# GNN layer pair on one core: attribute sums on GpSimd for the whole first half, GpSimd's share of the one-hots from set 44 on, and x's pieces and second half moved

## The chip, the cores and the metric

One Trainium2 chip, one core. The time is device microseconds of that core, the median of several executions; less is better. Engines: PE (TensorE, matmuls), PEld (its weight loads), DVE (VectorE), ACT (ScalarE), POOL (GpSimd), SP (SyncE, which issues DMAs).

## The reference

The inputs are x (3125 nodes, 64 channels), 53125 edges (src, dst, one attribute each) sorted by dst, and the weights of two message-passing layers. Cut to what matters:

```python
def _mp_layer(x, src, dst, edge_attr, W, b):
    loops = jnp.arange(n)
    src2, dst2 = concat([src, loops]), concat([dst, loops])
    ea2 = concat([edge_attr, zeros(n)])
    msg = concat([x[dst2], x[src2], ea2], axis=1) @ W + b
    return relu(segment_sum(msg, dst2, num_segments=n))
h = relu(_mp_layer(x, ..., W1, b1))
out = log_softmax(_mp_layer(h, ..., W2, b2))
return layernorm(x + out)
```

Since the message is linear, a layer needs, for each node, the sum of its neighbours' rows (an adjacency matrix times x), its degree, and the sum of the attributes of its edges.

## The kernel before

The 3125 nodes are 25 groups of 125. The adjacency matrix is built on the chip as 625 windows, each a 128x125 by 128x125 product on PE of two one-hot matrices made from the keys of 5 nodes' edges. Windows go in 79 **sets** of 8 (the last has one). One set is: DVE writes the one-hots of the set into one of three buffers `oh` (`onehots(k)`, L569: one compare of `iota_bank`, which lies in PSUM, with `keys`); PE builds the 8 windows in one of two PSUM buffers (`build(k)`, L1057); ACT copies them to the band of `adj` (`evacuate(k)`, L909). `build(k)` waits for set k-2's evacuation, `onehots(k)` for `build(k-3)`. PE runs four sets ahead: in its block b it does `build(b + 4)` and then layer 1's eight matmuls of set b (`layer1`, L1079). The order of all engines' work is written out by hand, by the set or block number.

Some work stands between the sets. When a group's 25 windows are summed, DVE reduces them (`reduce_sums`, L601); for each three groups there is an epilogue through the PSUM bank `epb`, started at the blocks in `TURN` (`turn_sums`, `hidden`, `messages` on PE; their copies on ACT; `scale_x`, `z_rest`, `z_low` on DVE). Layer 2 (L1126) starts when layer 1 is done, and needs nothing but PE and the final work on DVE.

What the change touches:

- **Shared one-hots.** From set `SHARED_FROM` = 12 on, DVE makes the one-hots of seven windows of a set (16 x 126 columns become 14 x 126) and GpSimd those of the eighth (`last_onehot`, two instructions of L441). PE waits for it ahead of the eighth matmul.
- **Attribute sums.** 625 blocks of edges are held as 125 rows by 5 columns j. For each j, DVE makes five masked sums (`attr_sums`, L556: one instruction with accumulation each), at the sets in `SUM_SET`. They need the distances `d_f` of that j, which ACT makes (`distances`, at the blocks in `DIST_BLOCK`). SP stores the five sums to DRAM and loads them turned (L1258, L1261), GpSimd splits them in bf16 parts (`split_sums`, at the sets in `SPLIT_BLOCK`), and `turn_sums` on PE waits for them (`se_parts`): for part 1 at block 21, part 2 at 29, part 3 at 41, part 4 at 60, part 5 at 69.
- **x's pieces.** Layer 1 takes x as three bf16 pieces: high (`cast_x`, ACT), middle (`rest_of_x` on DVE, then `cast_middle_x` on ACT), low (`low_of_x`, DVE). This is done for two halves of the groups, 12 and 13. Layer 1's first matmul waits for the first half's low piece, the thirteenth for the second half's.
- **Gathers.** GpSimd issues five indirect DMAs for the edges (L400) and five for the attributes (L404), each when its offsets are known (`off_ready`).
- **The bias rows** are split in three parts as well (`cast_bias`, `bias_rest`), and nine small DMAs on SP (L1253) copy them to their place; in SP's order they stand ahead of the first store of attribute sums.

## Time and profile before

| | |
|---|---|
| median of 3 runs | 193.68 us (193.29 to 193.81) |
| the profiled execution | 193.38 us, of which the span of its instructions is 191.3 us |
| PE busy | 173.1 us (90%) |
| PEld busy | 157.6 us (82%) |
| DVE busy | 161.4 us (84%) |
| ACT busy | 114.1 us (60%) |
| POOL busy | 98.6 us (52%) |
| mean granted clock of PE | 0.979 of full speed |

Busy times are instructions' spans. PE's matmuls are pipelined and their ends are modelled, so that the start of one instruction to the start of the next tells more than a length; the same holds for GpSimd. Times in rows are from the span's start. The profiled execution takes 2.1 us more than its span, and is 0.3 us below the median.

### The profile page before, as it was taken

Reading aid. Unit: us, or ns where it says so; the run is one execution under the profiler, and the core shown is the slowest. Engines: PE = TensorE matmul, PEld = TensorE weight load, DVE = VectorE, ACT = ScalarE, POOL = GpSimd, SP = SyncE. Lnnn points to the kernel's source line nnn. Section 1 sums busy time; section 2 is a strip of 40 time slices with the busy share of each in tenths; the row PEclk is TensorE's granted clock in tenths of the full one; section 3 lists DMA queues with packets and bytes.
Section 4 is the critical chain, followed back from the end, with each engine's and each line's share of the span. In section 5 each row is a group of like instructions: output and inputs, shape, how many; then the busy total and the mean of one; then the engine's idle time right before and its main releaser. Section 6 shows DMA issues by size and latency. Waiting matters only on the chain.

```text
span 191.3 us, 5193 instructions
## 1 busy us (share of the span) xinstructions
PE 173.1 (90%) x2050; PEld 157.6 (82%) x2051; DVE 161.4 (84%) x407; ACT 114.1 (60%) x197; POOL 98.6 (52%) x192
## 2 busy tenths in 40 slices
PE   7686587999999999999999999999999999999940
PEld 2133376998899987999999999999999999999930
DVE  0989999999999999999979979729429969888773
ACT  2526897888888989999989989863311102012201
POOL 6388504799889988988999989500000000000000
PEclk9969999999999999999999999999999999999995
DMA  1336200000000000000000000000000010200010
GB/s 45 103 90 146 65 11 2 6 1 4 1 6 1 4 1 4 2 4 1 3 0 3 2 3 0 3 0 5 0 3 2 16 27 0 44 13 17 20 25 20
DMA packets 9032, 3.35 MB, mean 18 GB/s; under 512 B 8240, under 2 KB 8557, under 8 KB 9007
## 3 DMA queue, kind: packets, MB, share of 16 engines
q1 hardware_dynamic: 8207, 2.08, 5.3%
q0 software_dynamic: 800, 0.93, 2.2%
q8 instruction: 17, 0.28, 0.7%
q14 instruction: 8, 0.07, 0.1%
HBM read 2.18 MB, written 0.81 MB: 16 GB/s over the span
## 4 chain that ended last, share of the span: by engine, by line
PE 64%; DVE 26%; DMA 5%; issue 3%; ACT 1%; DVEq 0%
PE pset L1126 18%; PE acc L1079 18%; DVE oh L569 16%; PE pset L1057 11%; PE acc L1126 9%; PE epb L1109 3%; PE epb L1120 3%; DMA adj<-in_edges,adj 3%; DMA adj<-in_dst 2%; DVE adj L556 1%; PE epb L1097 1%; DVE u L601 1%; DVE adj L581 1%; DVE x L586 1%; PE epb L1111 1%
## 5 line engine op out<-in xcount | busy, mean ns | idle before, releaser
L441 POOL TENSOR_SCALAR oh<-iota,keys 128x125 bf16<-128x125 bf16 x132 | 78.2, 615 | 14.9 <-PE pset L1057 14.3
L909 ACT ACTIVATE adj<-pset 125x1000 bf16<-125x1000 f32 (+1 forms) x79 | 78.4, 996 | 10.0 <-PE pset L1057 7.2
L569 DVE TENSOR_TENSOR oh<-iota_bank,keys 128x1764 bf16<-128x1764 bf16 (+4 forms) x81 | 83.1, 1051 | 0.4 <-PE pset L1057 0.3
L1079 PE MATMUL acc<-x,adj 125*125 125x195 bf16 x625 | 65.4, 248 | 0.3 <-DVE x L586 0.3
L1079 PEld LDWEIGHTS acc<-x,adj 125*125 125x125 bf16 x625 | 54.7, 136 | 0.9 <-issue 0.5
L1057 PE MATMUL pset<-oh 128*128 128x125 bf16 x625 | 47.3, 218 | 6.8 <-DVE oh L569 4.8
L1057 PEld LDWEIGHTS pset<-oh 128*128 128x128 bf16 x625 | 38.6, 97 | 10.4 <-ACT adj L909 6.1
L1126 PE MATMUL pset<-z,adj 125*125 125x192 bf16 x425 | 36.8, 246 | 0.0
L1126 PEld LDWEIGHTS pset<-z,adj 125*125 125x125 bf16 x425 | 35.5, 136 | 0.1
L988 ACT ACTIVATE x<-x 125x192 f32<-125x192 f32 (+2 forms) x6 | 2.6, 427 | 32.4 <-DVE x L737 32.4
L1126 PE MATMUL acc<-z,adj 125*125 125x192 bf16 x200 | 17.5, 246 | 0.0
L1126 PEld LDWEIGHTS acc<-z,adj 125*125 125x125 bf16 x200 | 16.8, 136 | 0.0
L601 DVE TENSOR_REDUCE u<-acc 125x65 f32<-125x195 f32 x25 | 8.9, 354 | 6.9 <-PE acc L1079 6.7
L1027 PE MATMUL acc<-adj 128*128 128x512 bf16 x31 | 11.3, 526 | 1.2 <-DVE adj L492 1.2
L1027 PEld LDWEIGHTS acc<-adj 128*128 128x128 bf16 x32 | 4.0, 127 | 6.5 <-issue 4.4
L400 POOL DMA_INDIRECT adj<-in_edges,adj x5 | 6.3, 1270 | 4.6 <-DVE adj L519 3.3
L728 DVE TENSOR_REDUCE x<-pset 125x64 f32<-125x192 f32 x17 | 5.4, 351 | 3.5 <-PE pset L1126 3.4
L556 DVE SCALAR_TENSOR_TENSOR adj<-adj 125x128 bf16<-125x128 f32 x25 | 7.4, 297 | 0.0
L404 POOL DMA_INDIRECT adj<-in_edge_attr,adj x5 | 6.1, 1211 | 1.5 <-issue 1.5
L1109 PE MATMUL epb<-turn,w1c 128*128 128x375 f32 x16 | 6.8, 506 | 0.0
L1120 PE MATMUL epb<-w2c,turn 128*125 128x128 f32 x48 | 6.7, 277 | 0.0
L622 DVE TENSOR_TENSOR u<-epb,z 125x192 f32<-125x192 f32 (+1 forms) x9 | 3.0, 338 | 4.1 <-ACT z L936 4.1
(125 smaller groups left out, 150.5 us busy)
## 6 DMA issues: line engine op xcount, KB each, us to landing
x_nat<-in_x_tiles SPq DMA_DIRECT2D x1, 406.2 KB
x_nat<-in_x_tiles SPq DMA_DIRECT2D x1, 375.0 KB
out<-x SPq DMA_DIRECT2D x2, 187.5 KB
out<-x SPq DMA_DIRECT2D x3, 93.8 KB
adj<-in_dst SPq DMA_DIRECT2D x1, 208.5 KB
bw<-adj SPq DMA_DIRECT2D x9, 1.0 KB
out<-x SPq DMA_DIRECT2D x1, 125.0 KB
adj<-in_edges,adj POOLq DMA_INDIRECT x5, 4.9
```

The lines of the kernel that those rows point to most:

```text
L400: gp.indirect_dma_start(pairs[:, j, 0:2 * (SLOTS - LOOPS)], None, edges, bass.IndirectOffsetOnAxis(off_idx[:, j:j + 1], 0)).then_inc(pairs ...
L441: ins = gp.tensor_scalar(oh[k % 3][:, OWN, side, 0:Q], iota1[:, 0:Q], keys[:, place(k * SET + OWN), side, 0:1], None, ALU.is_equal)
L556: dve.scalar_tensor_tensor(out=se_junk[:, j * WD + r, :], in0=d_f[:, j, :], scalar=float(r), in1=attrs[:, j, :], op0=ALU.is_equal, op1=ALU ...
L569: ins = dve.tensor_tensor(out=oh[k % 3][:, at_w:at_w + m, :, 0:2 * PAIRS].rearrange("p w t (q e) -> p (w t) q e", e=2), in0=iota_p.unsquee ...
L601: dve.tensor_reduce(u[i % 2][:, m, C:2 * C + 1], acc[g % 2][0:Q, 0:XW].rearrange("p (t c) -> p c t", t=3), AX.X, ALU.add)\
L909: ins = act.activation(bands[c][0:Q, :, at_w:at_w + n * WD].rearrange("p h (w e) -> p h w e", e=WD), rows[:, 0:n, 0:WD * G].rearrange("p w ...
L1027: pe.matmul(acc[1][:, :], still[:, 0:128], still, start=True, stop=True)
L1057: ins = pe.matmul(pset[k % 2][:, i // 4, i % 4 * 128:i % 4 * 128 + WD * G], oh[k % 3][:, i, 0, :], oh[k % 3][:, i, 1, 0:Q], start=True, st ...
L1079: ins = pe.matmul(acc[g % 2][0:Q, 0:XW], block_of_adj(g, h), x3[:, h, 0:XW], start=(h == 0), stop=(h == G - 1))
L1109: pe.matmul(epb[:, 0, 0:n], w1c[:, :], flat(i)[:, 0:n], start=True, stop=False)
L1120: ins = pe.matmul(z_cols(b - a)[:, m, :], flat(i)[:, m * Q:(m + 1) * Q], w2c[:, :], start=True, stop=True)
L1126: ins = pe.matmul(bank2(g)[0:Q, :], block_of_adj(g, h), z3[:, h, :], start=(h == 0), stop=(h == G - 1))
```

## The change

GpSimd makes all attribute sums. For each j it makes five masks, multiplies all of them with the attributes, and halves the 5 x 128 products seven times; a semaphore (`mask_chain`) orders each step behind the one before. Its share of the one-hots begins with set 44 in place of 12, behind all sums and splits in its program; until then DVE makes whole sets. GpSimd also makes the low piece of x's first half, and the rest and the low piece of the second half, between its gathers. SP asks for x's second half when the third offset is known, ahead of the weights, not when the first gather has landed. ACT casts the second half ahead of its first evacuation, its middle piece ahead of the third one, and makes `q_f` for j = 0, which was DVE's. The bias parts move to later sets, and two of ACT's `distances` four blocks forward.

```diff
-DIST_BLOCK = {1: 2, 2: 14, 3: 28, 4: 34}
-SUM_SET = {0: 16, 1: 24, 2: 31, 3: 37, 4: 43}
+DIST_BLOCK = {1: 2, 2: 14, 3: 24, 4: 30}
-SHARED_FROM = 12
+SHARED_FROM = 44
-SPLIT_BLOCK = {0: 26, 1: 34, 2: 44, 3: 52, 4: 60}
@@ gpsimd
+            def rest_of_x(i, a, b):
...
+                gp.wait_ge(xs_ready, i + 1)
+                gp.tensor_tensor(x_rest[:, a:b, :], x_nat[:, a:b, :], x3[:, a:b, 0:C], ALU.subtract).then_inc(xs_rest, 1)
...
+            def low_of_x(i, a, b):
...
+                gp.wait_ge(xm_ready, i + 1)
+                gp.tensor_tensor(x3[:, a:b, 2 * XC:2 * XC + C], x_rest[:, a:b, :], x3[:, a:b, XC:XC + C], ALU.subtract)\
+                  .then_inc(xl_ready, 1)
...
             gather_edges(0)
+            gather_edges(1)
             gather_attrs(0)
-            gather_edges(1)
-            gather_attrs(1)
-            for j in range(2, J):
-                gather_edges(j)
-            for j in range(2, J):
+            low_of_x(0, 0, XA)
+            rest_of_x(1, XA, G)
+            gather_edges(2)
+            low_of_x(1, XA, G)
+            gather_edges(3)
+            gather_edges(4)
+            for j in range(1, J):
                 gather_attrs(j)
...
+            def attr_sums(j):
+                gp.wait_ge(attrs_in[j], 16)
+                if j:
+                    gp.wait_ge(dist_ready, j)
+                    gp.wait_ge(se_ready, j)
+                else:
+                    gp.wait_ge(key_ready, 1)
+                for r in range(WD):
+                    gp.tensor_scalar(se_mask[:, r, :], d_f[:, j, :], float(r), None, ALU.is_equal).then_inc(mask_chain, 1)
+                done = j * (WD + 7) + WD
+                gp.wait_ge(mask_chain, done)
+                gp.tensor_tensor(se_mask, se_mask, attrs[:, j:j + 1, :].broadcast_to([Q, WD, SLOTS]), ALU.mult).then_inc(mask_chain, 1)
+                for n in (64, 32, 16, 8, 4, 2):
+                    done += 1
+                    gp.wait_ge(mask_chain, done)
+                    gp.tensor_tensor(se_mask[:, :, 0:n], se_mask[:, :, 0:n], se_mask[:, :, n:2 * n], ALU.add).then_inc(mask_chain, 1)
+                gp.wait_ge(mask_chain, done + 1)
+                gp.tensor_tensor(se_w[:, j, :], se_mask[:, :, 0], se_mask[:, :, 1], ALU.add).then_inc(se_ready, 1)
+
+            attr_sums(0)
+            for j in range(J):
+                if j + 1 < J:
+                    attr_sums(j + 1)
+                split_sums(j)
             for k in range(NSETS):
-                for j in range(J):
-                    if k == SPLIT_BLOCK[j]:
-                        split_sums(j)
                 if shared(k):
                     last_onehot(k)
@@ vector
-            bias_rest(0)
...
-            low_of_x(0, 0, XA)
             onehots(4)
-            rest_of_x(1, XA, G)
...
-                if k == 6:
-                    low_of_x(1, XA, G)
-                if k == 9:
+                if k == 10:
+                    bias_rest(0)
+                if k == 14:
                     bias_rest(1)
...
-                for j in range(J):
-                    if 0 <= k - SUM_SET[j] < WD:
-                        attr_sums(j, k - SUM_SET[j], k - SUM_SET[j] + 1)
@@ scalar
-            cast_bias(0)
             cast_x(0, 0, XA)
+            act.wait_ge(pairs_in[0], 16)
+            act.wait_ge(loops_ready, 2)
+            act.activation(q_f[:, 0, :], pairs[:, 0, 0::2], ACT.Copy, scale=1.0 / Q, bias=-float(Q // 2) / Q).then_inc(q0_ready, 1)
...
+            cast_x(1, XA, G)
             evacuate(0)
             evacuate(1)
-            cast_x(1, XA, G)
+            cast_middle_x(1, XA, G)
...
-                if b == 0:
-                    cast_middle_x(1, XA, G)
                 if b == 2:
+                    cast_bias(0)
+                if b == 8:
                     cast_bias(1)
-                if b == 6:
+                if b == 12:
                     cast_bias(2)
@@ sync
             sp.dma_start(x_nat[:, 0:XA, :], x_tiles[:, 0:XA, :]).then_inc(xnat_in[0], 16)
+            sp.wait_ge(off_ready, 3)
+            sp.dma_start(x_nat[:, XA:G, :], x_tiles[:, XA:G, :]).then_inc(xnat_in[1], 16)
             sp.dma_start(w1c[:, :], W1[0:2 * C, :]).then_inc(w_in, 16)
...
-            sp.wait_ge(pairs_in[0], 16)
-            sp.dma_start(x_nat[:, XA:G, :], x_tiles[:, XA:G, :]).then_inc(xnat_in[1], 16)
...
-                    sp.wait_ge(se_ready, (j + 1) * WD)
+                    sp.wait_ge(se_ready, j + 1)
```

How the order of instructions moves is seen at three places. On GpSimd, behind the constants, stood in a row before (L400 edges, L404 attributes, L441 the shared one-hots):

```order
L400 DMA adj<-in_edges,adj 125x246 [waits off_ready]
L404 DMA adj<-in_edge_attr,adj 125x123
L400 DMA adj<-in_edges,adj 125x246 [waits off_ready]
L404 DMA adj<-in_edge_attr,adj 125x123
L400 DMA adj<-in_edges,adj 125x246 [waits off_ready] x3
L404 DMA adj<-in_edge_attr,adj 125x123 x3
L441 TENSOR_SCALAR oh<-iota,keys 128x125 [waits keys_ready,built]
```

Now there stand (L415 low piece, L410 rest of x, L468 to L477 one j's attribute sums):

```order
L400 DMA adj<-in_edges,adj 125x246 [waits off_ready] x2
L404 DMA adj<-in_edge_attr,adj 125x123
L415 TENSOR_TENSOR x<-adj,x 125x12x64 [waits xm_ready]
L410 TENSOR_TENSOR adj<-x_nat,x 125x832 [waits xs_ready]
L400 DMA adj<-in_edges,adj 125x246 [waits off_ready]
L415 TENSOR_TENSOR x<-adj,x 125x13x64 [waits xm_ready]
L400 DMA adj<-in_edges,adj 125x246 [waits off_ready] x2
L404 DMA adj<-in_edge_attr,adj 125x123 x4
L468 TENSOR_SCALAR adj<-adj 125x128 [waits key_ready,attrs_in0]
L468 TENSOR_SCALAR adj<-adj 125x128 x4
L471 TENSOR_TENSOR adj<-adj 125x640 [waits mask_chain]
```

Three passes over x have come between the gathers, and the sums follow where the shared one-hots began.

On GpSimd at set 44, before: a `split_sums` (L423 to L431) between shared one-hots of one set and the next.

```order
L441 TENSOR_SCALAR oh<-iota,keys 128x125
L423 CAST stats<-se 125x5x3 [waits se_in2]
L425 TENSOR_TENSOR se_rest<-se,stats 125x5 [waits se_chain]
L427 CAST stats<-se_rest 125x5x3 [waits se_chain]
L429 TENSOR_TENSOR se_rest<-se_rest,stats 125x5 [waits se_chain]
L431 CAST stats<-se_rest 125x5x3 [waits se_chain]
L441 TENSOR_SCALAR oh<-iota,keys 128x125 [waits built]
```

Now the last two splits (L437 to L445) stand ahead of the first shared one-hot, set 44's (L455):

```order
L437 CAST stats<-se 125x5x3 [waits se_in3]
L439 TENSOR_TENSOR se_rest<-se,stats 125x5 [waits se_chain]
L441 CAST stats<-se_rest 125x5x3 [waits se_chain]
L443 TENSOR_TENSOR se_rest<-se_rest,stats 125x5 [waits se_chain]
L445 CAST stats<-se_rest 125x5x3 [waits se_chain]
L437 CAST stats<-se 125x5x3 [waits se_in4]
L439 TENSOR_TENSOR se_rest<-se,stats 125x5 [waits se_chain]
L441 CAST stats<-se_rest 125x5x3 [waits se_chain]
L443 TENSOR_TENSOR se_rest<-se_rest,stats 125x5 [waits se_chain]
L445 CAST stats<-se_rest 125x5x3 [waits se_chain]
L455 TENSOR_SCALAR oh<-iota,keys 128x125 [waits keys_ready,built]
```

The wait for the fifth load (`se_in4`) is now ahead of every shared one-hot.

On ACT, around the first evacuations, before (L860 bias cast, L864 `cast_x`, L880 and L882 the keys, L868 `cast_middle_x`, L909 evacuation):

```order
L860 ACTIVATE adj<-adj 64x128 [waits b_in]
L864 ACTIVATE x<-x_nat 125x12x64 [waits xnat_in0]
L880 ACTIVATE keys<-acc 128x125x2 [waits keyt_done]
L882 ACTIVATE keys<-acc 128x125x2
L868 ACTIVATE x<-adj 125x12x64 [waits xs_rest]
L909 ACTIVATE adj<-pset 125x25x40 [waits built] x2
L864 ACTIVATE x<-x_nat 125x13x64 [waits xnat_in1]
L909 ACTIVATE adj<-pset 125x25x40 [waits built] x3
L868 ACTIVATE x<-adj 125x13x64 [waits xs_rest]
```

Now (L878 `cast_x`, L888 `q_f`, L898 and L900 the keys, L882 `cast_middle_x`, L927 evacuation):

```order
L878 ACTIVATE x<-x_nat 125x12x64 [waits xnat_in0]
L888 ACTIVATE adj<-adj 125x128 [waits loops_ready,pairs_in0]
L898 ACTIVATE keys<-acc 128x125x2 [waits keyt_done]
L900 ACTIVATE keys<-acc 128x125x2
L882 ACTIVATE x<-adj 125x12x64 [waits xs_rest]
L878 ACTIVATE x<-x_nat 125x13x64 [waits xnat_in1]
L927 ACTIVATE adj<-pset 125x25x40 [waits built] x2
L882 ACTIVATE x<-adj 125x13x64 [waits xs_rest]
L927 ACTIVATE adj<-pset 125x25x40 [waits built] x5
```

The cast of x's second half now waits ahead of the first evacuation, and the cast of its middle piece, which waits for GpSimd's pass L410, ahead of the third.

## Rows read from the trace of the kernel before

**Rows 1.** Busy time of each engine by stage: window, length, busy us (instructions), clock, DMA.

```profile
16.70:50.00 33.30, 27.16 (x355) 24.50 (x357) 33.10 (x55) 27.03 (x34) 21.99 (x35) 1.00 0.11 24
50.00:76.00 26.00, 25.55 (x316) 23.38 (x315) 25.54 (x65) 23.66 (x43) 23.16 (x45) 1.00 0.04 3
76.00:129.00 53.00, 53.00 (x697) 51.26 (x696) 45.48 (x80) 46.88 (x74) 42.74 (x83) 1.00 0.02 2
```

**Rows 2.** Waits in 16 to 76 us: engine and line, releaser, total us, times, longest.

```profile
PEld pset L1057 <- ACT adj L909: 6.1, 7, 1.6
PE pset L1057 <- DVE oh L569: 4.8, 11, 0.8
```

**Rows 3.** Timeline of PE: start, length, line, tile [idle before it]; the builds of sets 24, 44 and 45.

```profile
50.30 0.60 PE L1057 MATMUL pset<-oh 128*128 128x125 bf16 x8
...
80.17 0.60 PE L1057 MATMUL pset<-oh 128*128 128x125 bf16 x8
...
81.29 0.60 PE L1057 MATMUL pset<-oh 128*128 128x125 bf16 x8
```

**Rows 4.** Timeline of DVE, 14.8 to 20.8 us and 34 to 41 us.

```profile
14.79 0.29 DVE L593 TENSOR_TENSOR adj<-adj 64x128 f32<-64x128 f32 x1
...
15.38 4.55 DVE L569 TENSOR_TENSOR oh<-iota_bank,keys 128x2016 bf16<-128x2016 bf16 x4
19.84 0.98 DVE L586 TENSOR_TENSOR x<-adj,x 125x768 bf16<-125x768 f32 x1
20.75 1.19 DVE L569 TENSOR_TENSOR oh<-iota_bank,keys 128x2016 bf16<-128x2016 bf16 x1
...
34.49 3.03 DVE L569 TENSOR_TENSOR oh<-iota_bank,keys 128x1764 bf16<-128x1764 bf16 x3
...
39.33 1.06 DVE L569 TENSOR_TENSOR oh<-iota_bank,keys 128x1764 bf16<-128x1764 bf16 x1
...
40.53 1.06 DVE L569 TENSOR_TENSOR oh<-iota_bank,keys 128x1764 bf16<-128x1764 bf16 x1
```

**Rows 5.** Timeline of ACT, 14.9 to 22 us.

```profile
14.90 0.86 ACT L868 ACTIVATE x<-adj 125x768 bf16<-125x768 f32 x1
17.37 2.04 ACT L909 ACTIVATE adj<-pset 125x1000 bf16<-125x1000 f32 x2 [1.61 <-PE pset L1057]
19.30 0.89 ACT L864 ACTIVATE x<-x_nat 125x832 bf16<-125x832 f32 x1
20.09 1.89 ACT L909 ACTIVATE adj<-pset 125x1000 bf16<-125x1000 f32 x2
```

**Rows 6.** Timeline of POOL: a compare, a gather's issue, the pieces of split_sums.

```profile
1.73 0.29 POOL L379 TENSOR_SCALAR_AFFINE_SELECT ident<-ident 128x128 f32<-128x128 f32 x1 [0.16 <-POOL ident L377]
...
19.84 1.21 POOL L404 DMA_INDIRECT adj<-in_edge_attr,adj  x1 [0.30 <-issue]
...
49.30 0.21 POOL L423 CAST stats<-se 125x15 bf16<-125x15 f32 x1 [0.20 <-DMA se<-se_scratch]
...
61.27 0.20 POOL L425 TENSOR_TENSOR se_rest<-se,stats 125x5 f32<-125x5 f32 x1
61.55 0.21 POOL L427 CAST stats<-se_rest 125x15 bf16<-125x15 f32 x1
```

**Rows 7.** Timeline of SyncE's DMA queue: x's second half, the bias copies, the first store of attribute sums.

```profile
12.29 0.26 SPq L1244 DMA_DIRECT2D x_nat<-in_x_tiles  x1
...
33.62 5.64 SPq L1253 DMA_DIRECT2D bw<-adj  x9
44.61 0.27 SPq L1258 DMA_DIRECT2D se_scratch<-adj  x1
```

**Rows 8.** Groups by line: count, ns of one as least/median/most, first and last start.

```profile
L441 POOL TENSOR_SCALAR oh<-iota,keys x132: 590/604/802, 30.2 to 121.6; 128x125 bf16<-128x125 bf16 x132
...
L614 DVE TENSOR_TENSOR u<-x_nat,u x9: 225/408/513, 38.9 to 129.8; 125x192 f32<-125x192 f32 x8, 125x64 f32<-125x64 f32 x1
...
L556 DVE SCALAR_TENSOR_TENSOR adj<-adj x25: 271/279/478, 38.7 to 83.3; 125x128 bf16<-125x128 f32 x25
```

More of the change, by code:

```diff
@@ L159, in gnn @@
         se_w = tail([Q, J, WD], FP32)
-        se_junk = tail([Q, J * WD, SLOTS], BF16)
+        se_mask = tail([Q, WD, SLOTS], FP32)
         attrs = tail([Q, J, SLOTS], FP32)
@@ L185, in gnn @@
         scratch_band = free[0] // (G * Q) // BAND
-        assert scratch_band * BAND * G > (max(KEY_BLOCK[J - 1] + 4, SUM_SET[J - 1] + WD)) * SET
+        assert scratch_band * BAND * G > (KEY_BLOCK[J - 1] + 4) * SET
         keys = sb("keys", [128, 2 * Q, 2, 2], BF16)
@@ L320, in gnn @@
         keyt_done = sem("keyt_done")
+        q0_ready = sem("q0_ready")
         keys_ready = sem("keys_ready")
@@ L329, in gnn @@
         sech = sem("se_chain")
+        mask_chain = sem("mask_chain")
         se_parts = sem("se_parts")
@@ L534, in key_distances @@
                 dve.wait_ge(loops_ready, 2)
-                dve.tensor_scalar(d_f[:, j, :], pairs[:, j, 1::2], thr_neg[:, j:j + 1], None, ALU.add)
-                link(dve.tensor_scalar(q_f[:, j, :], pairs[:, j, 0::2], -float(Q // 2), 1.0 / Q, ALU.add, ALU.mult))
+                link(dve.tensor_scalar(d_f[:, j, :], pairs[:, j, 1::2], thr_neg[:, j:j + 1], None, ALU.add))
+                dve.wait_ge(q0_ready, 1)
             def key_tiles(j):
@@ L548, in key_sums @@
                                          op0=ALU.is_le, op1=ALU.mult).then_inc(key_ready, 1)
-            def attr_sums(j, r0, r1):
-                dve.wait_ge(attrs_in[j], 16)
-                if j:
-                    dve.wait_ge(dist_ready, j)
-                for r in range(r0, r1):
-                    dve.scalar_tensor_tensor(out=se_junk[:, j * WD + r, :], in0=d_f[:, j, :], scalar=float(r),
-                                             in1=attrs[:, j, :], op0=ALU.is_equal, op1=ALU.mult,
-                                             accum_out=se_w[:, j, r:r + 1]).then_inc(se_ready, 1)
             def onehots(k):
@@ L877, in copy_keys @@
                     act.wait_ge(oh_ready, done + 1)
-                    act.wait_ge(last_ready, done + 1 - SHARED_FROM)
+                    if done >= SHARED_FROM:
+                        act.wait_ge(last_ready, done + 1 - SHARED_FROM)
                 mine = slice(j % 2 * Q, (j % 2 + 1) * Q)
```

4 lines of the change are left out of this document (removed).

## The prediction

> **What bounds the kernel now.** I read the busy times by stage first [rows 1]. From 76 us to 129 us PE is busy for all 53 us, and layer 2 behind it needs PE alone: time saved ahead of 76 us reaches the end whole, and time saved on other engines behind it is worth nothing. From 16.7 to 50 us PE is idle for 33.3 - 27.2 = 6.1 us, from 50 to 76 us for 0.45 us, while DVE has 0.2 and 0.5 us to spare. So the stage in which the matrix is built is DVE's until about 50 us, and almost equally PE's and DVE's from there on. The waits say the same [rows 2]: before 76 us PE's builds wait for DVE's one-hots 11 times (4.8 us) and for ACT's evacuations 7 times (6.1 us), and those are late because the builds were. The clock is 1.00 in all these stages and plays no part. At most the 6.5 us of PE's gaps can be won.
>
> **What DVE is relieved of, and what it gets.** In full sets the starts of one-hots are (4.55 - 1.19) / 3 = 1.12 us apart, in shared sets (3.03 - 1.06) / 2 = 0.985 us; a set that becomes whole costs DVE 0.13 us [rows 4]. An attribute sum between two one-hots puts them 40.53 - 39.33 = 1.20 us apart, so it costs 1.20 - 0.985 = 0.215 us, less than its span of 0.28 [rows 4]. A pass over x costs 20.75 - 19.84 = 0.91 us from start to start; the 832-element ones I take at 0.93 [rows 4]. Until set 16, DVE loses three passes (2.77 us), the bias instruction ahead of the first one-hot (0.3 us; it comes back at set 10, but PE waits for the first one-hot first), and `q_f` (0.1 us, since ACT makes it beside `d_f`); it gets sets 12 to 16 whole, 5 x 0.13 = 0.65. It comes out 2.5 us ahead. By set 24 it has eight more whole sets (-1.04) and five sums less (+1.08): still 2.5. From set 24 to 44 the sums outweigh (17 x 0.215 = 3.65 against 19 x 0.13 = 2.47), and DVE alone would reach 3.7. But set 24 was built at 50.3 us [rows 3], and from there PE has only its own 0.45 us to give. So PE reaches set 44 about 2.5 + 0.4 = **2.9 us earlier**, if GpSimd is never waited for: set 44's build at 77.3 in place of 80.17, set 45's at 78.4 in place of 81.29 [rows 3]. ACT has 6.3 us free until 50 and 2.3 in 50 to 76 [rows 1]; its work is the same, so it follows.
>
> **The start.** Three things could hold the first sets.
> The second half of x is asked for when the third offset is known, at about 10.4 us in place of 12.29 [rows 7]. Its first reader before ran at 19.30 [rows 5], so the transfer takes at most 7.0 us. Now ACT wants it at 15.7, behind the cast of the first middle piece, and before the first evacuation, which could begin at 17.37 - 0.4 = 17.0. I take a landing at 16, cast done at 16.9: hidden. At the bound it lands at 17.4, the cast ends at 18.3 and the first evacuation is 1.3 us late.
> GpSimd's passes: two-input instructions of more than 5 elements don't show in the trace. The cost for each element lies between the compare L379, 0.29 us for 128 columns, of which a tiny instruction's 0.20 is fixed [rows 6]: 0.7 ns for one input, twice that, 1.4, for two; and the shared one-hot, 604 ns for 125 columns [rows 8]: (604 - 200) / 125 = 3.2 ns. Both are one-input work; with a second input to fetch I take 2.0, above the middle of what the first gives. Then low(1st) runs 15.8 (when the cast of [rows 5] ends) to 17.5, rest(2nd), 0.2 + 832 x 0.0020 = 1.87 us, to 19.4, ACT's middle cast to 20.3, and the third evacuation starts at 20.3, where before it started at 20.09 [rows 5]. The first layer-1 matmuls so come as early as before; but the next thing that stood there, DVE's late low piece, is gone, since GpSimd finishes it at 19.4 + 1.5 (a gather's issue [rows 6]) + 1.9 = 22.8. From there PE can do a set in 1.12 us [rows 3] until it has caught up with DVE, whose 2.5 us therefore stand. With 3.2 ns the third evacuation starts at 22.5 and the gain of 2.5 sinks to about 1.
>
> **GpSimd's deadline.** This is what the sum turns on. Let A be the time of one j's sums. Behind low(2nd) at 22.8 stand six gather issues of 1.51 us (31.9), then sums 0 and 1 (31.9 + 2A). SP can store the first only behind the nine bias copies, which take 5.64 us and now start after ACT's cast at block 12, about 38.3; before they started at 33.62, after block 6 [rows 7]. So the store goes at 44.0, 0.6 us earlier than before, and the split can start 49.30 - 44.61 = 4.7 us behind it [rows 6, 7], at 48.7, done at 50.05: five instructions of 0.28 start to start [rows 6], 1.35 us. `turn_sums` of block 21 wants it at about 50: a wait of a few tenths, which the three one-hot buffers take up. Then follow sums 2, split 1, sums 3, split 2, sums 4, and now the store and load of sum 4 (4.7) with split 3 inside it, split 4 (1.35), the shared one-hots of sets 44 and 45 (2.4 [rows 8]). Set 45's is done at 50.05 + 3A + 2 x 1.35 + 4.7 + 1.35 + 2.4 = **61.2 + 3A**. PE's eighth matmul of set 45 stands 0.4 us behind the build's start: it wants it at 78.8 in the 2.9 us gain, and had it at 81.7 before. No wait if A is below 5.9, no gain at all if A is above 6.8. What follows set 45 costs nothing, since GpSimd needs 1.2 us a set and PE 1.12 plus its epilogues.
> A: five masks of 128 columns, between 0.29 (the compare with immediates, fp32 [rows 6]) and 0.60 (the same instruction as the one-hot, but that has bf16 and a scalar from memory [rows 8]); I take 0.34, near the fp32 compare: 1.7. Eight steps behind a wait, 0.275 start to start for the tiny ones [rows 6]: 2.2. Their elements, 640 + 320 + 160 + 80 + 40 + 20 + 10 = 1270, at 2.0 ns: 2.54. A = **6.4** (ends: 1.45 + 2.2 + 1.8 = 5.5; 3.0 + 2.2 + 4.1 = 9.3). Set 45's one-hot comes at 80.5, PE loses 1.7 us, and 2.9 - 1.7 = 1.2 us remain: 193.4 - 1.2 = **192.2**. That is against the profiled execution; the median lies 0.3 us above it.
> A page bears on this without entering the sum: the Trainium skill's GPSIMD Engine Reference, Performance versus the Vector engine, gives 4497 ns for a two-input add over 2048 fp32 columns. An estimate from it is 2.2 ns an element, A = 6.7 and 192.9; no run here shows it yet.
> Everything behind set 48 is left alone: the evacuation of set 50, which waits for the last store, comes at 89 or so, and sum 4 is stored by 73.
>
> **The rivals.**
> *GpSimd is quick.* A below 5.9 (the lower ends for masks or elements): no wait at set 44, the whole 2.9 us: 190.5. For it speaks that the only fp32 compare takes 0.29; against it, that the one row of this very instruction takes twice that. Chance 0.25.
> *GpSimd is late.* This one ends on the other side. Masks at 0.60 alone give A = 7.7: set 45's at 84.3, 2.6 us later than before: 196.0. It decides from A = 6.8 up; at 9.3 with a slower start it would be 201. Chance 0.27.
> *The two engines block each other.* DVE's instructions with two SBUF inputs might hold up, or be held by, GpSimd's. Before, GpSimd's one-hots ran 590 to 802 ns, `scale_x` on DVE 408 to 513, the attribute sums 279 to 478 [rows 8]: at most 0.2 us once, nothing like the whole 0.6 us of the other instruction. Between 32 and 77 us DVE now has some 18 such instructions (nine of the keys, four scales, three low pieces, two bias rests). At 0.2 us each that is 3.6 us on DVE; with the 25 sums gone, which met the same, about 2 net: 194. If each waited for the rest of a GpSimd instruction of 1.5 us, half a microsecond on average, it would be 9 us and more than 199. Chance 0.06.
> The Trainium skill, SBUF — State Buffer, Who interferes with whom, says that such a pair excludes each other for a whole instruction. By that rule the last figure holds; rows 8 show 0.2.
> *x's second half lands late* (17.4): the start is 1.3 us late, of which DVE's lead over PE hides part: 193. Chance 0.04.
>
> **How the numbers follow.** Forecast (A from 5.9 to 6.7, net gain 0.3 to 2.9): 0.38. A difference under 0.3% (0.6 us) can't be told from none. Faster: quick 0.25, the forecast 0.31 of 0.38: 0.56. Within: 0.07 of the forecast, 0.03 of the late case, 0.03 of the others: 0.13. Slower: the other 0.31. The range goes from 190.2 (quick, a little more at the start) to 196.5 (A = 7.8); what is left out is the far end of the late and the blocking case, some 0.15, and little below.
>
> **What the profile would show.** GpSimd's L468 near 0.34 us and L471 near 1.5; L410 near 1.9; DVE's one-hots 1.12 apart up to set 43; PE's build of set 24 near 47.8; a wait of 1 to 2 us of PE's build for POOL L455 at 79 to 80 us and none later; PE without gaps from there. The prediction is wrong if L468 is at 0.6 (late), if the build of set 24 is not early, or if DVE's two-input instructions grow.

## The result, and the profile after

The changed kernel takes **198.31 us** (median of 5, 196.83 to 201.09; the longest was left out of the comparison as disturbed) beside 193.68 for the kernel before (193.29 to 194.12): a ratio of **1.0231, 95% interval 1.0195 to 1.0267**. The forecast was 192.2. The profiled execution took 199.22 us against 193.38, 5.84 us more.

Busy times by stage (columns as in [rows 1]):

```profile
16.70:50.00 33.30, 27.52 (x366) 25.11 (x365) 33.04 (x42) 27.29 (x39) 26.16 (x36) 1.00 0.11 23
50.00:76.00 26.00, 24.72 (x310) 22.73 (x308) 24.73 (x34) 22.83 (x42) 22.66 (x52) 1.00 0.06 3
76.00:129.00 53.00, 49.40 (x618) 47.56 (x616) 42.92 (x64) 42.86 (x66) 42.53 (x81) 0.94 0.01 2
```

Up to 50 us PE does 11 matmuls more than in [rows 1]: a small gain. By 76 us half of it is gone (676 in both stages together, 671 before). Behind 76 us, where PE had no gap, 3.6 us of idle time have come, and the clock, which was 1.00, is 0.94. PE's timeline, the builds of sets 24, 44, 45, 46 and 47, which answer to [rows 3], and `turn_sums` of block 21 (L1116):

```profile
49.15 0.60 PE L1076 MATMUL pset<-oh 128*128 128x125 bf16 x8
...
52.04 0.51 PE L1116 MATMUL epb<-ident,u 125*128 125x125 f32 x3 [0.44 <-issue]
...
79.69 0.55 PE L1076 MATMUL pset<-oh 128*128 128x125 bf16 x7
83.85 0.28 PE L1076 MATMUL pset<-oh 128*128 128x125 bf16 x1 [3.60 <-POOL oh L455]
...
85.23 1.05 PE L1076 MATMUL pset<-oh 128*128 128x125 bf16 x8
...
88.11 1.04 PE L1076 MATMUL pset<-oh 128*128 128x125 bf16 x8
...
90.65 0.55 PE L1076 MATMUL pset<-oh 128*128 128x125 bf16 x7
```

Read it from the top. Set 24 comes 1.15 us earlier than before (50.30), 0.49 of which is there from the first build on (16.24 us, before 16.73); set 44 comes 0.48 us earlier (80.17). Set 44's eighth matmul, the first that reads a one-hot of GpSimd's, then stands for 3.8 us. Behind that wait eight matmuls of a build last 1.05 us where they lasted 0.60. The smaller wait at 52.04 is the one that `turn_sums` has for the first split, which ends at 51.84 (below). It costs the lead 0.5 us: set 25 is 1.09 us ahead of the kernel before, set 26 0.56. The stages of PE (the third number from the end is the granted clock):

```profile
83.00:86.00 3.00, 2.15 (x17) 2.14 (x18) 1.01 (x2) 1.00 (x1) 3.00 (x6) 0.50 0.00 0
86.00:90.00 4.00, 4.00 (x32) 3.94 (x31) 3.24 (x7) 2.82 (x5) 3.15 (x7) 0.58 0.00 0
90.00:129.00 39.00, 39.00 (x515) 37.42 (x515) 33.83 (x49) 35.17 (x54) 33.26 (x57) 1.00 0.01 2
```

The engine had stood idle, and from then the clock was at its lower level (0.50, 1.2 GHz) until shortly before 90 us. Set 47 starts at 90.65, 6.80 us behind the end of the wait; the run with filled waits, below, needs 4.28 us for the same stretch at 1.00. The balance: 0.48 of lead, less 3.8 of wait, less 2.5 of clock, makes 5.8 us lost, which is the difference of the two profiled executions.

GpSimd's timeline: the first split, the sums of one j, the last split and the first shared one-hots (start, length, count [idle before]):

```profile
50.50 0.22 POOL L437 CAST stats<-se 125x15 bf16<-125x15 f32 x1 [4.08 <-DMA se<-se_scratch]
...
51.78 2.63 POOL L468 TENSOR_SCALAR adj<-adj 125x128 f32<-125x128 f32 x5
54.50 1.55 POOL L471 TENSOR_TENSOR adj<-adj 125x640 f32<-125x640 f32 x1
56.13 2.88 POOL L475 TENSOR_TENSOR adj<-adj 125x320 f32<-125x320 f32 x6
59.09 0.20 POOL L477 TENSOR_TENSOR adj<-adj 125x5 f32<-125x5 f32 x1
...
81.30 0.21 POOL L437 CAST stats<-se 125x15 bf16<-125x15 f32 x1 [3.14 <-DMA se<-se_scratch]
...
82.58 2.94 POOL L455 TENSOR_SCALAR oh<-iota,keys 128x125 bf16<-128x125 bf16 x5
```

One j's sums take 59.23 - 51.78 = 7.45 us (to the start of the next split), 2.63 of them in the masks. Two waits for the way through DRAM stand ahead of and behind the whole row of sums: 4.08 us ahead of the first split, 3.14 ahead of the last. SyncE's queue shows why the first is long (compare [rows 7]):

```profile
40.23 5.64 SPq L1272 DMA_DIRECT2D bw<-adj  x9
45.91 0.46 SPq L1277 DMA_DIRECT2D se_scratch<-adj  x1
```

The sums of j = 0 are stored at 45.91, behind nine bias copies.

Last, VectorE beside GpSimd at two places:

```profile
33.77 1.54 POOL L471 TENSOR_TENSOR adj<-adj 125x640 f32<-125x640 f32 x1
...
33.90 1.57 DVE L613 TENSOR_TENSOR adj<-adj 64x128 f32<-64x128 f32 x1
...
63.23 1.55 POOL L471 TENSOR_TENSOR adj<-adj 125x640 f32<-125x640 f32 x1
...
63.98 1.01 DVE L649 TENSOR_TENSOR z<-u,z 125x192 bf16<-125x192 f32 x1
65.03 0.91 DVE L634 TENSOR_TENSOR u<-x_nat,u 125x192 f32<-125x192 f32 x1
```

`bias_rest`, 0.29 us in [rows 4], lasts 1.57 and ends at 35.47, just behind the end of GpSimd's multiply (35.31). `z_low` (0.35 before) and `scale_x` (at most 0.51 before, 0.35 elsewhere) overlap a later multiply (63.23) and the addition behind it in the same way. Together 1.28 + 0.66 + 0.56 = 2.5 us of the engine that sets the pace.

### The profile page after: what moved, and what is told of

The parts are those of the page before. It is cut to its first block, busy times and chain, and to the rows that moved or that the text cites. A ratio compares the mean times of both kernels' runs of the same rounds, so it can differ in the third digit from the quotient of the medians.

```text
span 197.2 us, 5130 instructions
## 1 busy us (share of the span) xinstructions
PE 174.3 (88%) x2050; PEld 159.9 (81%) x2051; DVE 160.1 (81%) x353; ACT 113.9 (58%) x198; POOL 99.6 (51%) x196
## 4 chain that ended last, share of the span: by engine, by line
PE 55%; DVE 15%; POOL 13%; DMA 9%; issue 3%; SPq 3%; ACT 1%; POOLq 0%; DVEq 0%
PE pset L1145 18%; PE acc L1098 14%; DVE oh L595 9%; PE pset L1076 9%; PE acc L1145 8%; POOL adj L475 4%; POOL adj L468 4%; DMA se<-se_scratch 3%; SPq L1272 3%; POOL adj L471 2%; DMA adj<-in_edges,adj 2%; DMA adj<-in_dst 2%; PE epb L1139 2%; PE epb L1128 2%; DMA se_scratch<-adj 2%
## 5 line engine op out<-in xcount | busy, mean ns | idle before, releaser
L595 DVE TENSOR_TENSOR oh<-iota_bank,keys 128x2016 bf16<-128x2016 bf16 (+4 forms) x81 | 86.3, 1104 | 1.3 <-PE pset L1076 1.0
L927 ACT ACTIVATE adj<-pset 125x1000 bf16<-125x1000 f32 (+1 forms) x79 | 77.7, 995 | 14.0 <-PE pset L1076 11.8
L1098 PE MATMUL acc<-x,adj 125*125 125x195 bf16 x625 | 66.9, 252 | 0.3 <-ACT adj L927 0.3
L1076 PE MATMUL pset<-oh 128*128 128x125 bf16 x625 | 48.4, 220 | 10.4 <-DVE oh L595 5.5
L1098 PEld LDWEIGHTS acc<-x,adj 125*125 125x125 bf16 x625 | 56.1, 139 | 0.9 <-ACT adj L927 0.6
L1076 PEld LDWEIGHTS pset<-oh 128*128 128x128 bf16 x625 | 39.4, 99 | 13.9 <-ACT adj L927 4.9
L455 POOL TENSOR_SCALAR oh<-iota,keys 128x125 bf16<-128x125 bf16 x68 | 39.8, 608 | 5.6 <-PE pset L1076 5.4
L475 POOL TENSOR_TENSOR adj<-adj 125x320 f32<-125x320 f32 (+5 forms) x30 | 12.6, 421 | 2.4
L468 POOL TENSOR_SCALAR adj<-adj 125x128 f32<-125x128 f32 x25 | 12.8, 535 | 0.6 <-POOL adj L477 0.2
L1046 PE MATMUL acc<-adj 128*128 128x512 bf16 x31 | 9.8, 464 | 1.2 <-DVE adj L528 1.2
L400 POOL DMA_INDIRECT adj<-in_edges,adj x5 | 6.4, 1276 | 4.8 <-DVE adj L555 4.1
L471 POOL TENSOR_TENSOR adj<-adj 125x640 f32<-125x640 f32 x5 | 7.8, 1550 | 0.4
L404 POOL DMA_INDIRECT adj<-in_edge_attr,adj x5 | 6.0, 1208 | 1.5 <-issue 1.5
```

The lines of the kernel that those rows point to most:

```text
L455: ins = gp.tensor_scalar(oh[k % 3][:, OWN, side, 0:Q], iota1[:, 0:Q], keys[:, place(k * SET + OWN), side, 0:1], None, ALU.is_equal)
L468: gp.tensor_scalar(se_mask[:, r, :], d_f[:, j, :], float(r), None, ALU.is_equal).then_inc(mask_chain, 1)
L471: gp.tensor_tensor(se_mask, se_mask, attrs[:, j:j + 1, :].broadcast_to([Q, WD, SLOTS]), ALU.mult).then_inc(mask_chain, 1)
L475: gp.tensor_tensor(se_mask[:, :, 0:n], se_mask[:, :, 0:n], se_mask[:, :, n:2 * n], ALU.add).then_inc(mask_chain, 1)
L595: ins = dve.tensor_tensor(out=oh[k % 3][:, at_w:at_w + m, :, 0:2 * PAIRS].rearrange("p w t (q e) -> p (w t) q e", e=2), in0=iota_p.unsquee ...
L927: ins = act.activation(bands[c][0:Q, :, at_w:at_w + n * WD].rearrange("p h (w e) -> p h w e", e=WD), rows[:, 0:n, 0:WD * G].rearrange("p w ...
```

## The experiments

**1. The last two splits held back.** Nothing of GpSimd's waits for the last store and load ahead of set 44:

```diff
                 if j + 1 < J:
                     attr_sums(j + 1)
-                split_sums(j)
+                if j < 3:
+                    split_sums(j)
             for k in range(NSETS):
+                for j in (3, 4):
+                    if k == SPLIT_LATE[j]:      # {3: 52, 4: 60}
+                        split_sums(j)
                 if shared(k):
```

> The changed kernel, but GpSimd's last two splits stand at sets 52 and 60 of its loop, as before the change, and not ahead of set 44's shared one-hots. Theory (the load that GpSimd waits for ahead of set 44 makes PE wait 3.6 us, and the clock at 0.5 to 0.6 behind that wait costs 2.6 us more): set 44's shared one-hot is done at about 78 us, PE waits nowhere for it, the granted clock stays at 1.00 from 16 us on, and the time is 199.2 - 3.8 - 2.6 = 192.9 us (within 0.4), with the runs closer together than the 4.3 us of the changed kernel. Rival (the wait at 80 us only uncovers another limit, DVE's whole sets or the epilogues' sums): PE waits elsewhere and the time stays above 195. Rival (the low clock comes by itself there): the granted clock still falls near 84 us, time near 195.5.

Measured: 192.88 us (192.42 to 194.09), ratio **0.9987 [0.9969, 1.0004]**. GpSimd's and PE's timelines:

```profile
76.99 1.19 POOL L456 TENSOR_SCALAR oh<-iota,keys 128x125 bf16<-128x125 bf16 x2
```
```profile
81.06 0.60 PE L1081 MATMUL pset<-oh 128*128 128x125 bf16 x8
```

The first shared one-hot is made at 77.0 instead of 82.6, PE never waits for GpSimd, and the clock is 1.00 from 16 us on. The ratio falls from 1.0231 by 2.4%, 4.7 us: the whole loss was that wait with its consequences. But the gain that was forecast isn't there either: set 45's build at 81.06, 0.23 us earlier than in [rows 3]. The wait for the first split stays too (0.49 us ahead of L1121, this kernel's `turn_sums`, at 52.32).

**2. SyncE stores the first sums ahead of the bias copies.** The nine copies stand behind the load of j = 0:

```diff
-            sp.wait_ge(bp_ready, 3)
-            ... nine copies of bpart into bw
             for j in range(J):
                 sp.wait_ge(se_ready, j + 1)
                 ... store and load of j's sums
+                if j == 0:
+                    sp.wait_ge(bp_ready, 3)
+                    ... nine copies of bpart into bw
```

> The changed kernel, but SyncE stores and loads the first attribute sums ahead of the nine bias copies. Theory (GpSimd's chain up to set 44 is one row of work, which starts again only when the first load lands): GpSimd's wait of 4.1 us at 46 to 50 us goes, all its later work moves 4 us forward, set 44's shared one-hot is done at 79.7 in place of 83.8, PE's wait of 3.6 us and the low clock behind it are gone: 193 us. The bias copies then end at about 47 us, before the first epilogue at 52 wants them. Rival (GpSimd's end is set by the load of the fifth sums, behind PE's blocks): no change of set 44's time, 198. Rival (the bias copies become late): PE waits at the first epilogue, 195.

Measured: 195.30 us (194.06 to 195.62), ratio **1.0095 [1.0068, 1.0122]**. The wait ahead of the first split is gone (it starts at 46.16), but another has taken a part of its place. GpSimd's timeline, the masks of j = 3 and the last split, and PE's, `turn_sums` of block 21 and set 44's eighth matmul:

```profile
57.67 2.63 POOL L468 TENSOR_SCALAR adj<-adj 125x128 f32<-125x128 f32 x5 [1.39 <-issue]
...
78.57 0.21 POOL L437 CAST stats<-se 125x15 bf16<-125x15 f32 x1 [3.25 <-DMA se<-se_scratch]
```
```profile
51.22 0.48 PE L1116 MATMUL epb<-ident,u 125*128 125x125 f32 x3
...
81.13 0.29 PE L1076 MATMUL pset<-oh 128*128 128x125 bf16 x1 [2.60 <-POOL oh L455]
```

The sums of j = 3 want the distances that ACT makes behind block 24. Of 4.1 us, 2.7 reach set 44's one-hot, which still comes 2.6 us late; the mean clock was 0.71 in 82 to 86 us. The expectation missed this second wait. Something else is seen here: `turn_sums` has no wait, and set 44's build starts at 77.98, 2.19 us ahead of the kernel before and 1.71 ahead of the changed kernel, though `bias_rest` is held here as well (1.59 us). Of the 1.71 us, 0.2 are there at the first build, 0.5 are PE's wait for the first split, and 0.9 come of `z_low` and `scale_x`, which now fall beside GpSimd's shorter additions and last 0.57 and 0.41 us.

**3. Probes on VectorE, both inputs in SBUF.** Experiment 1 and, behind each of the sets 13 to 43, a subtraction of 63 columns whose result nobody reads:

```diff
                 onehots(k)
+                if 13 <= k < 44:
+                    dve.tensor_tensor(probe[:, k - 13, :], x_nat[:, 0, 0:PAIRS], x_nat[:, 1, 0:PAIRS], ALU.subtract)
```

> The first experiment's kernel with one more DVE instruction behind the one-hots of each of sets 13 to 43: it subtracts two rows of 63 fp32 in SBUF into a scratch row, 31 instructions of about 0.22 us when nothing holds them. Theory (a DVE instruction with two SBUF inputs is held until the end of a GpSimd instruction that is reading two): those that meet GpSimd's 1.55 us product or the larger additions last up to 1.7 us and end with them; the others last 0.22 to 0.45, also beside the masks. Rival (the holding is brief, 0.2 us at most, and the one bias instruction of 1.57 us was late for another reason): none above 0.45.

Measured (a single run): 197.35 us. The group of the 31 probes (least, median, most in ns), then the timeline at 41.7 and at 55.3 us:

```profile
L678 DVE TENSOR_TENSOR adj<-x_nat x31: 205/215/1409, 33.5 to 81.7; 125x63 bf16<-125x63 f32 x31
```
```profile
41.73 1.55 POOL L473 TENSOR_TENSOR adj<-adj 125x640 f32<-125x640 f32 x1
41.95 1.41 DVE L678 TENSOR_TENSOR adj<-x_nat 125x63 bf16<-125x63 f32 x1
...
54.09 1.64 POOL L470 TENSOR_SCALAR adj<-adj 125x128 f32<-125x128 f32 x3
...
55.28 0.29 DVE L678 TENSOR_TENSOR adj<-x_nat 125x63 bf16<-125x63 f32 x1
```

A probe that starts inside GpSimd's multiply ends 0.1 us behind it, whatever is left of it; five lasted 0.52 to 1.41 us, each beside a two-input instruction of GpSimd. Beside the one-input masks, 0.53 us each, they last 0.21 to 0.29.

**4. The twin with one input in PSUM.**

```diff
-                    dve.tensor_tensor(probe[:, k - 13, :], x_nat[:, 0, 0:PAIRS], x_nat[:, 1, 0:PAIRS], ALU.subtract)
+                    dve.tensor_tensor(probe[:, k - 13, :], iota_bank[0:Q, 0:PAIRS], x_nat[:, 1, 0:PAIRS], ALU.subtract)
```

> The twin of the run with probes: the same 31 subtractions of VectorE in the same places, with the first input in PSUM instead of SBUF, the second in SBUF. (The probes are added work and change no output.) If VectorE is held only where both of its inputs come from SBUF beside a two-input instruction of GpSimd, none of the 31 lasts over 0.35 us, where five of the twins lasted 0.5 to 1.4 us. Rival: any two-input instruction is held: some again last over 0.5 us.

Measured (a single run): 194.67 us. The group, and the timeline at 42 us:

```profile
L678 DVE TENSOR_TENSOR adj<-iota_bank,x_nat x31: 207/214/218, 33.2 to 78.9; 125x63 bf16<-125x63 f32 x31
```
```profile
42.06 1.54 POOL L473 TENSOR_TENSOR adj<-adj 125x640 f32<-125x640 f32 x1
42.91 0.22 DVE L678 TENSOR_TENSOR adj<-iota_bank,x_nat 125x63 bf16<-125x63 f32 x1
```

None is held. The whole one-hots, whose iota lies in PSUM, never were either (1.19 to 1.21 us in this run and in the changed kernel); `bias_rest` between them still was (1.33 us).

**5. Only x's part.** The kernel before, with x's passes on GpSimd and its second half asked for early; the sums and the shares stay where they were (VectorE, from set 12). The bias casts are at ACT's blocks 2, 4 and 6, `bias_rest` at sets 8 and 10.

```diff
 (against the changed kernel)
-SHARED_FROM = 44
+SHARED_FROM = 12
-            attr_sums(0)          # GpSimd
-            ...
+                for j in range(J):                        # VectorE, as before
+                    if 0 <= k - SUM_SET[j] < WD:
+                        attr_sums(j, k - SUM_SET[j], k - SUM_SET[j] + 1)
```

> The kernel before with only the part of the change around x (GpSimd's three passes between its gathers, the second half's early request, ACT's order, q_f on ACT), and the bias casts at ACT's blocks 2, 4 and 6; attribute sums and shared one-hots as before. Theory (this part gave 3.5 us of lead to DVE by set 10, and the rest of the change ate it): DVE leads by 3 us at set 12; set 24's build is some 2.5 us early and the time is 193.4 - 2.5 to 3 = 190.6 us, unless GpSimd's gathers, which now end at 31 us, hold up the first shared one-hot, which costs up to 1.5 of it. Rival (PE and ACT bound that stretch, DVE's lead is worth nothing): 193.

Measured: **190.76 us** (190.61 to 191.11), ratio **0.9872 [0.9852, 0.9891]**: faster than both kernels. Set 24's build on PE's timeline, 2.24 us earlier than in [rows 3] (0.91 of it from the first build on, which starts at 15.82 us):

```profile
48.06 0.60 PE L1069 MATMUL pset<-oh 128*128 128x125 bf16 x8
```

**6. Only the sums' part.** The kernel before, with GpSimd's sums, shares from set 44 and the splits held back as in experiment 1; x's passes, the bias instructions and the loads stay as before.

```diff
 (against the kernel before)
-SHARED_FROM = 12
+SHARED_FROM = 44
-                for j in range(J):                        # VectorE
-                    if 0 <= k - SUM_SET[j] < WD:
-                        attr_sums(j, k - SUM_SET[j], k - SUM_SET[j] + 1)
+            attr_sums(0)                                  # GpSimd, as in the change
+            ...
```

> The kernel before with only the sums' part of the change: GpSimd makes the attribute sums and shares one-hots from set 44 on (splits 3 and 4 at sets 52 and 60 of its loop, so that set 44 waits for nothing); x's pieces stay on VectorE and the bias's in their old places. If the two parts simply add, it costs what separates the run of x's part alone from the run with the splits held back, 192.88 - 190.76 = 2.1 us: 193.1 + 2.1 = 195.2 (194.5 to 196), and instructions of VectorE with two inputs in SBUF are held beside GpSimd's multiply. Rival: the sums' part by itself is worth nothing or a little (192.5 to 193.5), since VectorE makes 40 sums less of 0.215 us (8.6 us) for 32 sets with 0.13 us more (4.2 us), and the 2.1 us come only of the two parts together.

Measured: 193.53 us (192.93 to 194.01), ratio **1.0001 [0.9986, 1.0016]**. The rival holds: alone, the part is worth nothing and costs nothing. (Its 8.6 us for 40 sums are wrong: [rows 8] show 25, which are 5.4 us against the 4.2 of the whole sets.) So x's part gives 1.28%, the sums 0, and both together (experiment 1) 0.13%: 1.14% or 2.2 us are lost between them. The held instructions are the larger part of it: in experiment 1 they lose 1.28, 0.63 and 0.57 us as in the changed kernel; here the second `bias_rest` comes at 29.92, takes 0.29 us, and the other two lose 0.3 us together. PE's wait for the first split is the other part: 0.49 us in experiment 1, none here, where the split starts at 44.37. (Between experiments 1 and 5 the places of the bias instructions differ too, so this sum alone doesn't settle it.)

This run also shows the reverse. x's passes are still VectorE's here, and two of GpSimd's instructions start while one of them runs:

```profile
22.34 1.04 DVE L597 TENSOR_TENSOR adj<-x_nat,x 125x832 f32<-125x832 f32 x1
22.57 1.23 POOL L454 TENSOR_SCALAR adj<-adj 125x128 f32<-125x128 f32 x1
...
25.54 1.01 DVE L602 TENSOR_TENSOR x<-adj,x 125x832 bf16<-125x832 f32 x1
...
25.98 1.97 POOL L457 TENSOR_TENSOR adj<-adj 125x640 f32<-125x640 f32 x1
```

A mask, with one input, takes 1.23 us for 0.53, and the multiply 1.97 for 1.55: VectorE's two-input instruction, when it comes first, holds GpSimd's too.

**7. The wait of set 44 filled, 44 matmuls.** PE repeats a matmul into the place that its last matmul overwrites:

```diff
                     if shared(k) and i == OWN:
+                        for _ in range(FILL if k == SHARED_FROM else 0):        # 44
+                            pe.matmul(... place of i ..., ... one-hots of i - 1 ...)
                         pe.wait_ge(last_ready, k - SHARED_FROM + 1)
```

> The changed kernel, and in set 44 TensorE repeats one matmul 44 times (44 x 0.079 us = 3.5 us) into the place that its last matmul then overwrites, ahead of the wait for GpSimd's first shared one-hot. The output is the same. If the slow stretch behind the wait comes of TensorE standing idle, the granted clock stays above 0.95 from 80 to 90 us, build(45) starts 0.65 us after build(44)'s last matmul as in the kernel before, and the time falls by the 2.6 us that the low clock cost: 195.7 (195 to 196.5). Rival: the low clock has another cause or the 2.6 us are another wait: 197.5 or more.

Measured: 196.94 us (196.22 to 198.02), ratio 1.0177 [1.0147, 1.0207]. The clock was 1.00 from 16 us on, and set 45 starts at 85.10. The repeated matmuls took 2.58 us, so 1.1 us stayed idle, after which no slow stretch followed.

**8. Short pieces.** Experiment 1, with the multiply and the first addition in five instructions each:

```diff
-                gp.tensor_tensor(se_mask, se_mask, attrs[:, j:j + 1, :].broadcast_to([Q, WD, SLOTS]), ALU.mult)
+                for r in range(WD):
+                    gp.tensor_tensor(se_mask[:, r, :], se_mask[:, r, :], attrs[:, j, :], ALU.mult)
                 ... the addition of 64 columns likewise
```

> The changed kernel with splits 3 and 4 held back (192.88), and GpSimd's multiply over 640 elements and its first addition over 320 in five instructions each, one for a distance, so that none of those has more than 128 elements (about 0.4 us). If VectorE's lost time comes of being held to the end of these two-input instructions, none of its short instructions lasts over 0.6 us from 16 to 76 us, the second bias_rest 0.3 instead of 1.57, build(24) starts about 1.2 us earlier (49.4 to 48.2), and the time is 191.7 (191.2 to 192.3). Rival: as much time is lost in small pieces, or another engine takes up the lead behind set 24: 192.5 to 193.3.

Measured: 194.84 us (193.57 to 195.44), ratio 1.0052 [1.0026, 1.0077]. The time missed, the mechanism didn't (set 24's build comes at 48.87, 0.5 us earlier than in experiment 1 and not 1.2). VectorE's timeline, the second `bias_rest` and `z_low`, and PE's, sets 44 and 45:

```profile
34.17 0.40 DVE L623 TENSOR_TENSOR adj<-adj 64x128 f32<-64x128 f32 x1
...
63.07 0.35 DVE L659 TENSOR_TENSOR z<-u,z 125x192 bf16<-125x192 f32 x1
```
```profile
77.79 0.55 PE L1086 MATMUL pset<-oh 128*128 128x125 bf16 x7
80.48 0.23 PE L1086 MATMUL pset<-oh 128*128 128x125 bf16 x1 [2.14 <-POOL oh L456]
...
81.22 0.64 PE L1086 MATMUL pset<-oh 128*128 128x125 bf16 x8
```

The holds are nearly gone (the longest instruction left has 0.65 us) and set 44 comes at 77.79, 2.4 us earlier than before the change. But eight more instructions lengthen one j's sums to 8.6 to 8.8 us, the first shared one-hot comes at 79.24, and PE waits 2.14 us, with a mean clock of 0.85 in 79 to 83 us and 0.63 in 83 to 86. The expectation had left out GpSimd's own time.

**9. Short pieces, shares from set 48.** `SHARED_FROM = 48` in experiment 8.

> The run with short pieces, and GpSimd shares one-hots from set 48 instead of 44, so that build(44) waits for nothing of GpSimd, which is done with its sums at 79.1 us there. In that run no instruction of VectorE was held over 0.65 us and build(44) came 1.9 us earlier than in the run with splits held back (77.79), but stood 2.14 us for the first shared one-hot and then at a low clock. If that wait ate the gain, it comes out here: four more whole sets cost VectorE at most 4 x 0.13 = 0.5 us, so 1.2 to 1.9 us under the run with splits held back, a ratio to the kernel before of 0.990 (0.987 to 0.993), 191.7 against 193.6. Rival: the lead of sets 24 to 44 is not passed on to the end: a ratio of 0.996 or more.

Measured: **191.18 us** (190.9 to 191.35), ratio **0.9891 [0.9870, 0.9912]**. Set 45's build stands at 79.42, PE doesn't wait for the first split (GpSimd starts it at 49.95, 0.84 us earlier than in experiment 1), and the stage behind 76 us is without a gap:

```profile
76.00:83.00 7.00, 7.00 (x94) 6.61 (x93) 6.93 (x12) 6.46 (x11) 5.74 (x15) 1.00 0.01 0
```

**10. The wait filled, 62 matmuls.** `FILL = 62` in experiment 7.

> As the run that fills the wait of set 44, with 62 repeated matmuls instead of 44, since those 44 took 2.58 us and not 3.5 and 1.1 us of idle time remained. At 0.059 us each they fill the wait. If the whole slow stretch comes of the idle time and the first run already avoided it, the time is the same as there within 0.3%, and 2.0 us (1.0%) under the changed kernel of the same chip. Rival: the repeated matmuls help little by themselves: within 0.3% of the changed kernel.

Measured: 196.53 us (196.19 to 196.92), ratio 1.0177 [1.0158, 1.0195]. PE's timeline, the repeated matmuls, set 44's last, and sets 45 and 47:

```profile
80.11 3.57 PE L1077 MATMUL pset<-oh 128*128 128x125 bf16 x62
83.58 0.23 PE L1080 MATMUL pset<-oh 128*128 128x125 bf16 x1
...
84.32 0.64 PE L1080 MATMUL pset<-oh 128*128 128x125 bf16 x8
...
87.86 0.60 PE L1080 MATMUL pset<-oh 128*128 128x125 bf16 x8
```

**11. The changed kernel again**, on the chip of experiments 9 and 10.

> The changed kernel as it is, timed on the chip of this batch, so that the filled waits can be compared with it directly: a ratio of 1.023 (1.0195 to 1.0267) to the kernel before, and again about 3.6 us of wait in set 44 and 2.5 us at a low clock behind it.

Measured: 198.60 us (197.58 to 198.99), ratio 1.0280 [1.0256, 1.0305], the wait as before:

```profile
83.65 0.29 PE L1076 MATMUL pset<-oh 128*128 128x125 bf16 x1 [3.36 <-POOL oh L455]
```

Set 47 starts at 89.17 here, 5.52 us behind the end of the wait: 1.2 us more than with the wait filled, where the first profiled execution lost 2.5. Timed on this chip, 62 useless matmuls in the wait save 198.60 - 196.53 = 2.1 us.

**All runs beside each other.** Start of set 45's build on PE and span of the profiled execution, both as differences from the kernel before (81.29 and 191.3 us):

| kernel | set 45's build | span | clock under 1.00 in 79 to 90 us |
|---|---|---|---|
| x's part alone (5) | -2.23 | -2.2 | no |
| short pieces, from 48 (9) | -1.87 | -1.9 | no |
| splits held back (1) | -0.23 | -0.2 | no |
| sums' part alone (6) | -0.08 | -0.1 | no |
| wait filled, 62 (10) | +3.03 | +3.1 | no |
| wait filled, 44 (7) | +3.81 | +3.8 | no |
| short pieces (8) | -0.07 | +1.5 | yes |
| store first (2) | +1.23 | +2.0 | yes |
| changed kernel again (11) | +3.75 | +4.4 | yes |
| changed kernel | +3.94 | +5.9 | yes |

Where the clock stayed, what set 45 has lost or won is lost or won at the end, to 0.1 us. Where it fell, 0.6 to 2.0 us more are lost behind set 45. (A place read from one execution also holds how early its first build began: 16.73 us before, 15.82 in (5), 17.24 in (6). What a part is worth is told by the timed ratios.)

## Why the prediction was wrong

The miss against the profiled execution is 199.22 - 192.2 = 7.0 us: 2.4 of lead that set 44 didn't have (2.9 forecast, 0.48 found), 2.1 of longer wait for GpSimd (1.7 forecast, 3.8 found), 2.5 of clock. The forecast was a gain; each of these three terms is larger than the 1.2 us that it left.

- **What bounds the kernel**: right. The table above shows it: time gained or lost up to set 45 reaches the end whole.
- **"The clock ... plays no part"**: the step that failed outright. It was read off stages in which PE never stood long. The forecast itself put a wait into the one stretch that had none, and priced it at its length. Filling the wait with matmuls (10, beside 11) gave back 2.1 us of the timed difference; of the rivals, none had this term.
- **"DVE comes out 2.5 us ahead"** at set 16. The costs in it were right: behind the start, VectorE's timeline has ten one-hots in one row, 1.12 us apart, and set 10's is made 3.5 us earlier than before.

```profile
14.89 11.24 DVE L595 TENSOR_TENSOR oh<-iota_bank,keys 128x2016 bf16<-128x2016 bf16 x10 [0.27 <-ACT keys L900]
...
26.77 1.20 DVE L595 TENSOR_TENSOR oh<-iota_bank,keys 128x2016 bf16<-128x2016 bf16 x1
```

  Then both `bias_rest` come back (0.6 us; the forecast had counted the first of them as won for good), the whole sets cost 0.65, and GpSimd's multiply holds the second `bias_rest` for 1.28. So 1.0 us is left at set 16, and 1.15 are found at set 24.
- **"2.9 us earlier"** at set 44: from set 24 on the sums were to outweigh the whole sets by 1.2 us, of which PE could take 0.4. Two more held instructions (1.22 us) and PE's wait for the first split (0.5 us between sets 25 and 26) took more than that. The forecast named this wait, "a wait of a few tenths, which the three one-hot buffers take up": they didn't. Where the first split came early (2), the lead lost nothing there and grew to 2.19. The holds are the rival **"the two engines block each other"**, with a chance of 0.06. It was dismissed with [rows 8], and that reading is the failed step: GpSimd's instructions there are one-hots, with one input. The two-input instructions that the change adds to GpSimd had no row before, so rows 8 said nothing about them. The price of the rival by its own rule (9 us, all 18 instructions) was as wrong: the three that started inside the multiply or the first addition were held, the others hardly. What the holds cost the kernel isn't measured by itself. From 0.9987 (1) to 0.9891 (9) it is 1.9 us, but in (9) PE's wait for the first split is gone too (0.5 us), since the bias copies start 0.9 us earlier, and four sets more are whole.
- **The start**: right. x's second half landed by 16.2 us, GpSimd's pass of 832 elements took 1.77 us for 1.87, and the first layer-1 matmul came at 21.7 us.
- **"A = 6.4"**: mis-sized; it is 7.45, above the break-even of 6.8 that the text gave. The masks cost 0.53 us apiece and not 0.34, 0.95 us of the 1.0. The 1270 elements at 2.0 ns were right (1.55 us for 640 with 0.2 fixed is 2.1), the eight steps too. The forecast took for the masks the row that was like them in type (L379, fp32, but a TENSOR_SCALAR_AFFINE_SELECT) and not the one that was like them in kind (L441, a TENSOR_SCALAR as they are).
- **The first split "at 48.7"**: 50.50, since the bias copies began at 40.23 and not at 38.3, behind `bias_rest` and ACT's cast. 1.8 + 3 x 1.0 = 4.8 us, less 0.4 for splits and a last load that were a little shorter, make set 45's shared one-hot come at 84.9 instead of 80.5. This was the rival **"GpSimd is late"** (0.27): the right case, its place and its sign, and its 196.0 for A = 7.7 is short by the holds and the clock.
- **"What follows set 45 costs nothing"**: right for GpSimd, which PE never waits for again, wrong by the clock.

On the page that bore on A: from the 4497 ns that the Trainium skill's GPSIMD Engine Reference, Performance versus the Vector engine, gives for a two-input add over 2048 fp32 columns, 2.2 ns an element is an estimate; the trace has 2.1.

On the other: the Trainium skill, SBUF — State Buffer, Who interferes with whom, says that a VectorE instruction with two SBUF inputs contends with a GpSimd one that reads SBUF, calls this an exclusive lock, and says that the order of issue decides who blocks. The multiply and the first addition agree (1.57 us for 0.29), the twin with one input in PSUM too (at most 0.218 us in 31 places), and so does the reverse in experiment 6, even for a mask with one input (1.23 us for 0.53). A mask that comes first doesn't agree: the probe at 55.28, with 0.45 us of the mask to go, lasted 0.29.

What stays open: why the low clock lasted longer in one profiled execution of the changed kernel than in the other (0.58 in 86 to 90 us, and 0.94), and why a mask that comes first hardly holds VectorE, when VectorE holds a mask. Moving `bias_rest` alone, off the multiply, wasn't tried, so that the holds and PE's wait for the first split have no price each.
